# Self-attention lead-in on one Trainium2 core: 50-row keys, a two-row fill, reordered values, fillers and first maxima

## The reference

```python
x_norm = modulate(_ln(x), shift_a, scale_a)          # (B, N, 256), here B=2, N=1024
qkv = x_norm @ W_qkv + b_qkv
q, k, v = jnp.split(qkv, 3, axis=-1)                 # 16 heads of 16
attn_w = jax.nn.softmax(jnp.einsum('bhqd,bhkd->bhqk', q, k) * scale, axis=-1)
attn_out = jnp.einsum('bhqk,bhkd->bhqd', attn_w, v)
attn_out = attn_out @ W_proj + b_proj
x = x + gate_a[:, None] * attn_out
```

## Time and profile before

| what | us |
|---|---|
| median of 3 runs | 1583.03 (1581.65 to 1585.23) |
| the profiled execution's own time | 1584.41 |
| its span, first to last instruction | 1582.6 |
| PE busy | 1461.1 (92%) |
| DVE busy | 1057.9 (67%) |
| ACT busy | 767.6 (49%) |
| POOL busy | 399.2 (25%) |
| share of PE in the chain that ended last | 64% |
| share of DVE in it | 26% |

### The profile page before, as it was taken

How to read it: one execution, slowest core, us unless ns; L and a number is a source line. 1 busy time by engine, 2 the same in 40 slices (tenths; PEclk the granted TensorE clock), 3 DMA queues, 4 the chain that set the end, 5 groups by cost and what they waited for, 6 DMA issues and landing times.

```text
span 1582.6 us, 26526 instructions
## 1 busy us (share of the span) xinstructions
PE 1461.1 (92%) x10481; PEld 920.4 (58%) x10481; DVE 1057.9 (67%) x2994; ACT 767.6 (49%) x1248; POOL 399.2 (25%) x451
## 2 busy tenths in 40 slices
PE   5889999999999999978998999899999999997798
PEld 3457664444455857656774767444445485765586
DVE  2574455899747446899457534689993744679953
ACT  1335432788834533325543542278885353332554
POOL 4420024642134010114123000654211600001320
PEclk9999997999999999999999999979999999999999
DMA  9500045221020000000140001722102000000000
GB/s 334 175 0 1 0 91 110 42 42 22 2 80 1 1 1 3 1 1 1 33 141 1 1 1 24 167 48 37 31 3 81 1 1 0 2 2 1 1 1 27
DMA packets 41631, 59.82 MB, mean 38 GB/s; under 512 B 10867, under 2 KB 30611, under 8 KB 40611
## 3 DMA queue, kind: packets, MB, share of 16 engines
q1 hardware_dynamic: 25239, 34.71, 7.1%
q0 software_dynamic: 13488, 16.06, 6.1%
q10 hardware_dynamic: 2780, 7.36, 1.3%
HBM read 42.22 MB, written 2.10 MB: 28 GB/s over the span
## 4 chain that ended last, share of the span: by engine, by line
PE 64%; DVE 26%; ACT 3%; issue 3%; DMA 2%; POOL 1%; ACTq 0%; DVEq 0%; POOLq 0%
PE ps L1038 8%; PE ps L1052 8%; PE ps L487 6%; PE ps L1396 4%; PE ps L897 4%; DVE taken L2475 3%; PE ps L1187 3%; DVE taken L2487 3%; DVE rs L2145 3%; PE ps L875 2%; PE ps L1421 2%; PE ps L1178 2%; DVE mm L2338 2%; PE ps L1023 2%; DVE mxw L2137 2%
## 5 line engine op out<-in xcount | busy, mean ns | idle before, releaser
L1713 ACT ACTIVATE pt<-ps 128x512 f32<-128x512 f32 x512 | 274.6, 595 | 67.7 <-PE ps L1038 53.1
L2338 DVE TENSOR_REDUCE mm<-ps 128x1 f32<-128x1024 f32 x240 | 288.6, 1222 | 26.5 <-PE ps L1023 24.0
L1038 PE MATMUL ps<-qx,kx 64*128 64x512 f32 x512 | 191.6, 465 | 2.5 <-DMA qx<-mxT 1.7
L2593 POOL TENSOR_TENSOR rstd<-ve,minus_half 128x4 f32<-128x4 f32 x32 | 35.0, 1094 | 612.5 <-DVE ve L2009 612.4
L1023 PE MATMUL ps<-kx,qx 48*128 48x512 f32 x480 | 183.6, 464 | 1.2 <-DVE mm L2338 1.1
L1052 PE MATMUL ps<-pt,v 128*32 128x256 f32 x2048 | 159.0, 395 | 0.1
L1038 PEld LDWEIGHTS ps<-qx,kx 64*128 64x128 f32 x512 | 81.5, 192 | 90.6 <-ACT pt L1713 69.7
L2222 DVE TENSOR_TENSOR rlo<-ring,rhi 128x512 fp32r<-128x512 f32 x48 | 33.1, 690 | 91.9 <-ACT ring L1665 91.9
L1052 PEld LDWEIGHTS ps<-pt,v 128*32 128x32 f32 x2048 | 44.5, 109 | 84.8 <-ACT pt L1713 56.6
L2640 POOL DMA_DIRECT2D qx<-mxT x64 | 35.7, 561 | 194.7 <-ACT mxT L1707 189.3
L1023 PEld LDWEIGHTS ps<-kx,qx 48*128 48x128 f32 x480 | 74.5, 194 | 15.3 <-DVE mm L2338 8.1
(11 more groups left out here) (379 smaller groups left out, 3399.5 us busy)
## 6 DMA issues: line engine op xcount, KB each, us to landing
wm<-in_L_xcond_W_mlp_dram SPq DMA_DIRECT2D x4, 1024.0 KB, 13.6
w3a<-in_L_xcond_w_m_dram SPq DMA_DIRECT2D x2, 2048.0 KB, 8.2
qx<-q_hi POOLq DMA_DIRECT2D x56, 64.0 KB, 2.3
kx<-k_hi POOLq DMA_DIRECT2D x56, 64.0 KB, 2.3
w<-in_L_xcond_e_w_dram SPq DMA_DIRECT2D x6, 512.0 KB, 7.7
w<-in_L_xcond_e_w_dram SPq DMA_DIRECT2D x2, 1536.0 KB, 13.1
s_ada<-in_L_xcond_w_ada_dram ACTq DMA_DIRECT2D x1, 2304.0 KB, 23.2
w3b<-in_L_xcond_w_m_dram SPq DMA_DIRECT2D x2, 1024.0 KB, 11.2
```

Of the source, the lines that this page charges most:

```text
L1038: pe.matmul(ps[:, bank, :], kx[r, p % 4, kc * P:(kc + 1) * P], qx[r, p % 4, half * 512:(half + 1) * 512], start=True, stop=True).then_inc( ...
L1713: act.activation(pt[:, n % 8, i * 512:(i + 1) * 512], ps[:, bank, :], ACT.Exp, scale=QK_SCALE).then_inc(st_read, 1)
L2338: return dve.tensor_reduce(mm[:, p % 2, e, t:t + 1], place().rearrange("p a q -> p (a q)"), X, ALU.max).then_inc(ring_read, 1)
```

## The change

It makes six edits, each in both batch rows:

- `key_scores` runs over 50 rows instead of 64. Rows 50 to 63 are not read any more, so the fill of `qx` (two DMAs of 16 x 4096) is dropped, and the fill of `kx` shrinks from 16 rows to two (2 x 3072 ahead of the lead-in, twice; 2 x 1024 later, twice).
- The two remaining early fill DMAs count on `first_ld`, for which m = 0 waits; the pieces of the second-half keys (k_hi and k_lo high) count on `fill_ld` instead.
- POOL no longer waits for `first_ld` ahead of the high pieces.
- `values` is issued one unit earlier: tile 0 stands ahead of m = 0's wait. The `full_step` pieces and the gate rows follow one unit earlier, too.
- The fillers begin at m = 11 instead of m = 12, and five more stand ahead of n = 0.
- ACT copies the first maxima ahead of the gates, not behind them.

```diff
-KA = 4 * HD
+KA = 3 * HD + 2
-N_FIRST = N_SPR + N_SPR // 2
+N_FIRST = N_SPR + 2 * 16
+N_FILL = N_SPR // 2 + 2 * 16
...
                 full_step(3)
+                values(1, (0,))
                 pe.wait_ge(v2_clear, b + 1)
...
                         if n == 0:
-                            pe.wait_ge(fill_ld, b * 96 + 64)
+                            keep_busy(5, 5)
                             pe.wait_ge(gates_ready, b + 1)
                         elif n == 6 * T:
-                            pe.wait_ge(fill_ld, b * 96 + 96)
+                            pe.wait_ge(fill_ld, b * N_FILL + N_FILL)
...
-                    if m == 12:
+                    if m == 11:
                         pe.wait_ge(full_ready, b * 4 + 4)
-                    if m >= 12 and n < 4:
+                    if m >= 11 and n < 4:
                         keep_busy(5 if n < 0 else 7, 2 if n < 0 else 1)
                     if m == 0:
-                        pe.wait_ge(first_ld, b * N_FIRST + N_SPR)
+                        pe.wait_ge(first_ld, b * N_FIRST + N_FIRST)
                     elif m == TB:
-                        pe.wait_ge(first_ld, b * N_FIRST + N_FIRST)
+                        pe.wait_ge(fill_ld, b * N_FILL + N_SPR // 2)
...
-                    if m < TB:
-                        values(1, (m,))
-                    elif m == 4:
+                    if m < TB - 1:
+                        values(1, (m + 1,))
+                    elif m == 3:
                         pe.wait_ge(full_ready, b * 4 + 1)
                         full_step(4, slice(0, 2 * P))
...
-                    elif m == 11:
+                    elif m == 10:
                         pe.wait_ge(full_ready, b * 4 + 3)
...
                 full_part(1, 1, 5)
+                maximum_rows(0)
                 act.wait_ge(gates_spread, b + 1)
...
-                    pool.dma_start(qx[64 * e + 3 * HD:64 * e + KA, :, :], g["c_fill"][0]).then_inc(fill_ld, 16)
-                    pool.dma_start(kx[64 * e + 3 * HD:64 * e + KA, 0:3, :], g["c_fill"][1, :, 0:3, :]).then_inc(fill_ld, 16)
+                    pool.dma_start(kx[64 * e + 3 * HD:64 * e + KA, 0:3, :], g["c_fill"][:, 0:3, :]).then_inc(first_ld, 16)
...
-                pool.wait_ge(first_ld, b * N_FIRST + N_SPR)
                 pool.wait_ge(hi_ready, b * 6 + 3)
-                pool.sem_inc(passed, 1)
-                part(1, 0, 0, high, first_ld)
+                part(1, 0, 0, high, fill_ld)
                 pool.wait_ge(ring_read, b * N_RING + 1)
-                part(1, 1, 0, high, first_ld)
+                part(1, 1, 0, high, fill_ld)
```

More of the change, by code:

```diff
@@ L1096, in _ @@
                     query_scores(q, at_m)
-                    if m < TB:
-                        values(1, (m,))
-                    elif m == 4:
+                    if m < TB - 1:
+                        values(1, (m + 1,))
+                    elif m == 3:
                         pe.wait_ge(full_ready, b * 4 + 1)
                         full_step(4, slice(0, 2 * P))
+                    elif m == 4:
+                        full_step(4, slice(2 * P, BLK))
+                        full_step(5, slice(0, 2 * P))
                     elif m == 5:
-                        full_step(5, slice(0, 2 * P))
-                        full_step(4, slice(2 * P, BLK))
+                        full_step(5, slice(2 * P, BLK))
                     elif m == 6:
-                        full_step(5, slice(2 * P, BLK))
-                    elif m == 7:
                         pe.wait_ge(v_ready, b * NB + NB)
                         full_step(6)
+                    elif m == 7:
+                        full_step(7, slice(0, 2 * P))
                     elif m == 8:
-                        full_step(7, slice(0, 2 * P))
-                    elif m == 9:
                         full_step(7, slice(2 * P, BLK))
-                    elif m == 11:
+                    elif m == 10:
                         pe.wait_ge(full_ready, b * 4 + 3)
@@ L1751, in _ @@
                                 probabilities(unit, i)
-                    if at_m == 9 and q < NP:
+                    if at_m == 9 and 1 <= q < NP:
                         maximum_rows(0)
@@ L2673, in _ @@
                 pool.wait_ge(v_done, b * NB + NB)
-                pool.wait_ge(fill_ld, b * 96 + 64)
+                pool.wait_ge(fill_ld, b * N_FILL + N_SPR // 2)
                 pool.sem_inc(passed, 1)
                 for e in range(2):
-                    pool.dma_start(kx[64 * e + 3 * HD:64 * e + KA, 3, :], g["c_fill"][1, :, 3, :]).then_inc(fill_ld, 16)
+                    pool.dma_start(kx[64 * e + 3 * HD:64 * e + KA, 3, :], g["c_fill"][:, 3, :]).then_inc(fill_ld, 16)
                 for p in range(NP):
@@ L2683, in _ @@
                         pool.wait_ge(full_ready, b * 4 + 4)
-                        pool.wait_ge(first_ld, (b + 1) * N_FIRST)
+                        pool.wait_ge(first_ld, b * N_FIRST + N_FIRST)
+                        pool.wait_ge(fill_ld, b * N_FILL + N_FILL)
                         pool.wait_ge(spread_ld[0], b * (N_SPR // 2 + 2 * N_SPR) + N_SPR // 2 + N_SPR)
@@ L2797, in constants @@
     ones_win[:, 1, HD:] = 1
-    fill = np.zeros((2, HD, 4, L), np.float32)
-    fill[1, 0:2] = -1
+    fill = np.full((2, 4, L), -1, np.float32)
     sel3 = np.zeros((P, E, P), np.float32)
```

## The result

The changed kernel takes 1574.49 us (median of 20 runs, 1560.41 to 1582.97) against 1584.40 us of the kernel before (median of 20, 1579.59 to 1588.73): ratio 0.9921, 95% interval 0.9900 to 0.9942, or 9.9 us less. The forecast was 1563 us, 19.9 us off the profiled execution of the kernel before. The sign was right, and the gain is half of what was forecast. A few executions of either kernel took 2002 to 2806 us and are left out of every comparison.

The account below looks back on a forecast made before the run. PE, busy nearly throughout, and lead-in losses reaching the end undiminished were taken as the bound. Row 0's 2.0 + 6.5 + 6.2 and row 1's 0.2 + 9.8, less 4.8, gave 19.9 us: 1564.5 profiled, median 1563, range 1554 to 1574.

Parts of the forecast that it names:

- rival 2: Lead-ins: clock drops in units 9 to 14, fillers do not restore it before values are weighed; 1574 us, chance 0.22.
- Small fill, idle at m = 0: Start of lead-ins: fill of 48 KB, not 896, lets weights and k_lo land earlier; gain 2.0 us row 0, 0.2 row 1.
- Two signs: Row 0 lead-in: q1 above 90% of the DMA engines from about 225 us; k_lo landing before 241.5 us.
- Clock at the start: Row 0, m = 0 to end of unit 13: without the idle, runs as row 1 did; gain 6.5 us.
- Maxima first: Row 1, first key scores: maxima copied about 2 us earlier, idle of 1.7 us goes; worth is the clock.
- Clock at the end: End of unit 13 to unit 24: full clock gains 6.2 us row 0, 9.8 row 1; short falls lose 2.4 each.
- 1.2 GHz for over 10 us of either lead-in: Either lead-in: the prediction's stated sign that it is wrong; no size in time.
- rival 1: Both lead-ins: full clock throughout, without the 4.8 us loss; 1556 to 1558 us, chance 0.25.
- a middle that no run took: Both lead-ins: one short fall per batch row, 2.4 us each; 1560 to 1567 us, chance 0.45.
- The premise of that step: Row 0, fall at 264 us: brought down by a thin stretch of 48-row scores, not by an idle.
- The five fillers at nothing: Ahead of n = 0: 1.1 us at full clock, beside DVE's reductions, priced at nothing; 2.9 us if clock is low.
- The rule weighed: Lead-ins: the skill lays clock falls on gaps where PE idles; by it the change would keep full clock, as in rival 1.

Follow-up runs that it names:

- e5: The changed kernel again, unaltered, on the chip of e6 to e8: 1561.03 us (4 runs).
- e3: The kernel before with the small fill alone (50 rows, two-row fill of kx, no fill of qx): 1576.73 us, ratio 0.9949.
- e8: e1 with the fill of 896 KB and 64-row key scores again, values tile still ahead of the wait: 1567.59 us.
- e7: e1 with the copy of the maxima behind the two gate copies again: 1562.69 us.
- e4: The changed kernel without the five fillers ahead of n = 0: 1560.85 us (6 runs).
- e9: The changed kernel without any filler ahead of n = 0 (six at m = 11 to 13 and the five go): 1574.22 us, ratio 0.9932.
- e10: The changed kernel again, unaltered, on one chip with e9 and e11: 1572.33 us, ratio 0.9903.
- e11: e1 again, on one chip with e9 and e10: 1562.78 us, ratio 0.9858.
- e12: e1 with the values tiles behind the scores again, tile 0 behind m = 0 and nothing ahead of the wait: 1564.50 us, ratio 0.9874.
- e1: The changed kernel plus five fillers in the thin units, one each at m = 7, 8, 10 and two at m = 9: 1562.08 us, ratio 0.9861.
- e6: e1 without the five fillers ahead of n = 0: 1561.22 us (4 runs).
- e2: The kernel before plus five fillers, at m = 8, 9, 10 (two) and 11, order of gates and maxima unchanged: 1584.54 us, ratio 1.0006.

## Why the prediction was right in sign and wrong in size

Its terms against the profiled execution of the change:

| term | forecast | in the profile |
|---|---|---|
| idle at m = 0, row 0 | 2.0 | 3.09 - 0.86 = 2.2 |
| m = 0 to the end of unit 13, row 0 | 6.5 | 26.4 - 21.9 = 4.5 |
| end of unit 13 to unit 24, row 0 | 6.2 less 2.4 | 19.2 - 23.8 = -4.6 |
| idle at m = 0, row 1 | 0.2 | 1.25 - 0.86 = 0.4 |
| m = 0 to the end of unit 13, row 1 | 0 | 19.9 - 20.0 = -0.1 |
| end of unit 13 to unit 24, row 1 | 9.8 less 2.4 | 22.8 - 14.6 = 8.2 |
| sum | 19.9 | 10.6 |

The profiled execution is 1584.4 - 1573.0 = 11.4 us shorter. Nearly all of the miss, 3.8 + 4.6 = 8.4 of 9.3 us, is in the third line of the table: the fall in batch row 0.

The stated range, 1554 to 1574 us, was reckoned from the 1583.03 us of three runs; from the 1584.40 of twenty its upper end is 1575.4. The median lies just inside, at rival 2's price, and that is luck in part: it holds because 13 of these 20 runs had one fall. On e5's occasion the same kernel has a median of 1561.

- **Small fill, idle at m = 0:** right in mechanism and size; e3 has it alone and e8 takes it back. Two signs were missed: q1 held 42% of the DMA engines, not 90%, and k_lo landed at 238.6 + 4.1 = 242.7 us, not before 241.5, because this execution ran 1.8 us late there (238.6 against 236.8 us at the issue). By the estimate 237.2 + 4.1 it would have been 241.3. In row 1 the term was too small in one sense: e8 shows that the big fill would have cost 2.2 us there, with POOL's pieces issued as in the change.
- **Clock at the start:** right. Full clock at 244 to 248 us.
- **Maxima first:** the idle of 1.7 us did go, but not by this edit alone, as I had put it: e7 undoes the copy's place at no cost. With the copy in its old place, the gates a unit earlier do most of it and the fillers ahead of n = 0 the rest (e7). With the copy first, no fillers are needed: e4 and e9 have none of the five and no wait ahead of n = 0.
- **Clock at the end, the step that failed:** "Behind it, however, PE now has fillers at m = 11, 12, 13 and five more, dense work that should bring the clock back soon", priced at 2.4 us per batch row. The fall came where the text put it, but the fillers did not end it: it lasted 27 us, and its price measured 13.0 us in e10's groups (12.6 between the medians of the two groups of the first 20 runs), where 2.4 was put down. By the prediction's own sign, 1.2 GHz for over 10 us of either lead-in, it was wrong here. In its place the runs of the change show all or nothing for each batch row: no fall, 1561 us; one, 1574; two, as the clock of a single run suggests, 1583. The prediction had both as rivals 1 and 2 and put the most chance on a middle that no run took. Rival 2's picture (clock down in units 9 to 14, not back before values are weighed) is what batch row 0 did in the first profile, rival 1's is what row 1 did; in e10's profile it was the other way round. Their mix was missed: I gave one outcome to both rows and to all runs.
- **The premise of that step.** "No idle brought it down, but a thin stretch of 48-row scores" was put as a finding. The rows that the prediction had show the fall at 264 us behind such a stretch, not that the stretch was the cause; e9 against e11 supports it, and e12's falls are of another kind.
- **The five fillers at nothing:** mis-sized. "Beside DVE's reductions of units 11 to 13" they are not: e10's row 0 takes 34.1 us to unit 24 and e4's 32.6, so they cost 1.5 us per batch row at full clock. That is most of why the end of unit 13 to unit 24 took 14.6 us in row 1 and not 13.0.
- **Price of a fall.** 11.1 of the 13.0 us are between DVE's first reduction and unit 24, in both profiles of the change. Where the rest lies stays open.
- **The rule weighed.** By gaps in which PE idles the change would have kept full clock. The traces of the change, e3 and e9 disagree: clock down with no gap over 0.48 us (the change), 0.47 (e9) and 0.23 (e3) between m = 0 and the fall. The Trainium skill, "TensorE: Matmul & The Clock Gate", section "A second HAM failure mode: psum-queue depth-cycling", says that frequent micro-idles between groups of matmuls, in a cycle through PSUM banks, can make the clock oscillate too. Its cause fits the place, PE waiting on DVE's ring of two; what it would make of the time differs, since no run here oscillates in the lead-in: a long fall stays for 24 to 27 us. Thin work and micro-idles are not told apart by the long falls, because a filler removes both; the short falls of e12 came without either.

**The version that beats both** is e1 (e11): 1562.08 and 1562.78 us, 22 us under the kernel before; 9.6 us under the change in the one group where both ran and the change fell (the intervals just meet), and close to the change where it did not fall (e5 to e7). e6, without the five fillers, is as fast, and 1.5 us per batch row shorter by its trace. Nine runs of e1 and e11 show no long fall by their clocks (0.982 and above), against falls in 4 of 6 runs of the change in e10 and in 14 of 20 in the first timing. The eight runs of e6 and e7 have none either, but they say little, since the change had none on their occasion. The clock alone is a coarse sign: a run of e12 with two short falls has 0.981.

## What to carry to other kernels

Where a median lies between two groups of runs, read the mean granted clock of every run before explaining the median: one profile shows only one of the outcomes. In a stage that another engine paces, put fillers into the thin stretch itself, ahead of the place where the clock would fall; fillers behind it did not bring the clock back here and lay on the path at half speed. Price them at full clock from a trace, too: a median of a few runs did not show the 1.5 us per batch row that five cost. And remove the waits first: fillers in front of a wait that stays bought nothing (e2).

## What the runs showed of the hardware that was not expected

- The clock fell with no gap over 0.48 us in PE's row behind m = 0 (the change; 0.23 us in e3), in a stream of 48-row matmuls, and stayed at 1.2 GHz for 24 to 27 us in which PE's row reads 4.00 of 4 us busy; it came back when the weighing of values (x34 matmuls in 4 us) was under way.
- Each of the long falls that began without a wait (before, the change, e3, e9, e10; seven in all) began within 2 us behind the first of the three gate-row matmuls. e1 and e11 have the same matmuls at the same unit and no fall, so these alone do not do it.
- The same kernel with the same data falls or not from run to run, and the share differs by occasion: 14 of 20 runs, 0 of 4, 4 of 6.
- An idle of 2.17 us ahead of m = 0 took the clock down in batch row 0 of e8, and one of 2.19 us, in row 1, did not: the length of a wait alone does not tell.
- In e12 PE had no gap from 244 to 272 us, and the clock fell all the same; this fall, behind the first key scores, was over in 7 us. Whether its later place made it short was not tested.
